# A decoder's quantised feed-forward on one Trainium2 core: int16 roundings, a stationary column of maxima, columns by token half, and constant products in TensorE's rests

## What is computed

```python
def _L0_ffn_ref(x, w_gate, w_up, w_down):        # x: 1024 tokens x 128
    def act_qdq(x):                              # one scale for the whole tensor
        qmax = 2.0 ** (ACT_BITS - 1) - 1.0       # 32767
        scale = jnp.maximum(jnp.max(jnp.abs(x)) / qmax, 1e-12)
        return jnp.clip(jnp.round(x / scale), -qmax - 1.0, qmax) * scale
    def fixed_qdq_u16(x):
        scale = 1.0 / 65536.0
        return jnp.clip(jnp.round(x / scale), 0.0, 65535.0) * scale
    x = act_qdq(x)
    up = act_qdq(x @ lpbq_dequant(w_up).T)       # 384 x 1024 results
    gate = act_qdq(x @ lpbq_dequant(w_gate).T)
    sig = fixed_qdq_u16(jax.nn.sigmoid(gate))
    gate = act_qdq(gate * sig)
    o = act_qdq(gate * up)
    return o @ lpbq_dequant(w_down).T
```

## Time and profile before

| | |
|---|---|
| median of 3 runs | 481.63 us (478.5 to 483.13) |
| the profiled execution's own time | 481.88 us |
| its span (first to last instruction) | 480.1 us |
| VectorE busy | 335.9 us, 70% |
| TensorE busy | 320.3 us, 67% |
| ScalarE busy | 194.4 us, 40% |
| mean granted TensorE clock | 0.83 |

### The profile page before, as it was taken

One profiled execution on the slowest core, in us unless ns is written; L12 is line 12 of the kernel. 1 busy time (PEld: TensorE's weight loads), 2 busy tenths in 40 slices (PEclk: granted clock), 3 DMA queues, 4 the chain that ended last, 5 costly groups with the idle time before them and its releaser, 6 DMA issues.

```text
span 480.1 us, 8901 instructions
## 1 busy us (share of the span) xinstructions
PE 320.3 (67%) x3651; PEld 197.5 (41%) x3651; DVE 335.9 (70%) x479; ACT 194.4 (40%) x310; POOL 90.0 (19%) x86
## 2 busy tenths in 40 slices
PE   2605779767666575799999973920095998789821
PEld 0201233222222334477777761400033777467710
DVE  0796899999999955666666644488833674666574
ACT  1519968546445330122222252475113442434420
POOL 0070033444343403400000000000003341112000
PEclk9856799888899597699999996765576798989965
DMA  8600000000005768100000000000000000000001
GB/s 236 255 0 16 1 1 22 23 22 22 1 21 101 132 117 286 73 3 1 3 1 3 3 1 0 0 0 1 0 0 0 3 4 3 1 2 5 3 0 44
DMA packets 22500, 16.91 MB, mean 35 GB/s; under 512 B 17216, under 2 KB 20416, under 8 KB 22336
## 3 DMA queue, kind: packets, MB, share of 16 engines
q1 hardware_dynamic: 22464, 16.39, 12.5%
HBM read 11.67 MB, written 4.72 MB: 34 GB/s over the span
## 4 chain that ended last, share of the span: by engine, by line
PE 36%; DVE 19%; SPq 6%; issue 5%; ACT 3%; DMA 1%; POOL 0%; DVEq 0%; ACTq 0%; POOLq 0%
PE psum L441 29%; SPq L423 6%; PE psum L699 3%; DVE small L1455 2%; DVE arena_a L1397 2%; PE psum L581 2%; PE psum L548 2%; DVE small L1539 1%; DVE arena_a L1417 1%; ACT arena_b L1050 1%; DMA g_scratch<-arena_a 1%; DVE arena_b L1510 1%; DVE arena_b L1516 1%; DVE arena_b L1543 1%; DVE xc L1220 1%
## 5 line engine op out<-in xcount | busy, mean ns | idle before, releaser
L441 PE MATMUL psum<-arena_b 64*64 64x9 f32 (+2 forms) x1348 | 75.3, 278 | 43.8 <-DVE arena_b L1364 30.6
L441 PEld LDWEIGHTS psum<-arena_b 64*64 64x64 f32 (+2 forms) x1348 | 34.9, 141 | 73.6 <-issue 38.8
L441 PE MATMUL psum<-arena_a 64*64 64x64 f32 (+2 forms) x1056 | 34.8, 235 | 9.0 <-ACT arena_a L904 5.4
L1539 DVE TENSOR_REDUCE small<-psum 128x16 f32<-128x1024 f32 x16 | 19.6, 1225 | 20.2 <-PE psum L441 20.2
L441 PEld LDWEIGHTS psum<-arena_a 64*64 64x64 f32 (+1 forms) x1056 | 21.9, 139 | 28.5 <-issue 15.8
L1148 POOL TENSOR_TENSOR arena_b<-arena_b 128x512 f32<-128x512 f32 x16 | 24.8, 1551 | 43.3 <-DVE arena_b L1334 43.3
L441 PE MATMUL psum<-arena_a,xw 128*128 128x128 f32 x256 | 31.1, 279 | 2.4 <-ACT arena_a L969 2.2
L441 PEld LDWEIGHTS psum<-arena_a,xw 128*128 128x128 f32 x256 | 30.1, 195 | 4.0 <-ACT arena_a L969 2.7
L441 PE MATMUL psum<-arena_b,const 32*128 32x128 f32 (+1 forms) x138 | 9.1, 346 | 32.3 <-DVE arena_b L1462 32.0
L1172 POOL MEMSET arena_b<- 128x16 f32 x4 | 0.3, 128 | 160.1 <-DVE x L1529 160.1
L1145 POOL TENSOR_TENSOR arena_b<-arena_b 128x512 f32<-128x512 f32 x16 | 21.9, 1369 | 44.0 <-DVE arena_b L1351 44.0
(11 more groups left out here) (218 smaller groups left out, 731.1 us busy)
## 6 DMA issues: line engine op xcount, KB each, us to landing
g_scratch<-arena_a SPq DMA_DIRECT2D x16, 256.0 KB, 6.6
logg<-g_scratch SPq DMA_DIRECT2D x1, 3584.0 KB, 13.2
xw<-in_xw SPq DMA_DIRECT2D x1, 2048.0 KB, 9.1
arena_b<-in_rkvo SPq DMA_DIRECT2D x8, 192.0 KB, 2.3
ffn_w<-in_ffn SPq DMA_DIRECT2D x1, 576.0 KB, 10.8
x<-in_xT SPq DMA_DIRECT2D x2, 256.0 KB, 3.0
arena_a<-in_boxes SPq DMA_DIRECT2D x8, 64.0 KB, 4.0
arena_b<-in_rkvo SPq DMA_DIRECT2D x8, 64.0 KB, 1.9
```

Source lines behind the costliest of these rows:

```text
L441: return nc.tensor.matmul(o, l, r, start=start, stop=stop, **kw)
L1539: v_.tensor_reduce(mx.rearrange("p (r h) -> p r h", r=4), s4, axis=AX.X, op=ALU.max).then_inc(s.a_max, 1)
```

## The change

Five edits, all in the feed-forward.

1. The roundings of gate, up and gate times sigmoid are single passes that write int16; the scaled sigmoid is written as uint16. The multiplies read these integers and write float32. Four integer tensors lie in an area of SBUF that the cross attention has left.
2. The broadcast uses the column of maxima itself, repeated 128 times, as stationary operand and the identity as moving operand. `f_diag` and its pass are gone. In `scale_of` a one-column operation before the broadcast (`per`) takes the factor in; all rounds then have the same three operations behind the reduce.
3. Columns are ordered by token half first: piece h * 3 + j. The first three gate products need only half 0 of x, whose subtraction VectorE makes; ScalarE makes half 1's.
4. VectorE reduces the gate's products from PSUM, and ScalarE copies a bank after VectorE is done with it. Up is reduced in one pass over 3072 columns. The down products start chunk by chunk, half 1's roundings are all ScalarE's, and the last scale is applied in the residual add.
5. `keep_running(n)` issues n products of constants (mean matrix by 512 columns of `xw`) into `pD`'s first bank, which nothing reads then: 3 before round 0's broadcast, 2 behind it, 4 before round 2's, 2 before rounds 3 and 4, 1 behind round 4's.

```diff
@@ tensor @@
             def spread_max(n):
                 pe.wait_ge(s.f_amax, n + 1)
-                mm(pD[:, 512:640], mean_w, f_diag).then_inc(s.f_bc, 1)
+                mm(pD[:, 512:640], small[:, 0:1].to_broadcast([P, P]), ident).then_inc(s.f_bc, 1)
+
+            def keep_running(n):
+                for _ in range(n):
+                    mm(half(pD, 0), mean_w, xw[:, 0:512])
+
+            keep_running(3)
             spread_max(0)
-            pe.wait_ge(s.f_q3, 1)
+            keep_running(2)
...
-                    mm(banks[j], ffn_wT[:, (k * HID + j // 2) * P:(k * HID + j // 2 + 1) * P],
-                       half(fx, j % 2)).then_inc(s.h_psum, 1)
+                    elif j == 0:
+                        pe.wait_ge(s.fx_done, 1)
+                    elif j == HID:
+                        pe.wait_ge(s.fx1_done, 1)
+                    w = k * HID + j % HID
+                    mm(banks[j], ffn_wT[:, w * P:(w + 1) * P], half(fx, j // HID)).then_inc(s.h_psum, 1)
...
-            for n in range(2, 5):
-                spread_max(n)
-            for h in range(2):
-                pe.wait_ge(s.h_o, h + 1)
+            keep_running(4)
+            spread_max(2)
+            pe.wait_ge(s.f_mid, 1)
+            keep_running(2)
+            spread_max(3)
+            pe.wait_ge(s.f_mid, 3)
+            keep_running(2)
+            spread_max(4)
+            keep_running(1)
+            for h in range(2):
                 for j in range(HID):
...
+                    pe.wait_ge(s.h_o1 if h else s.h_o, j + 1)
@@ scalar @@
+            act.wait_ge(s.fx_big, 2)
+            nc.scalar.activation(half(fx, 1), half(fx, 1), ACT.Identity, bias=der[:, 30:31]).then_inc(s.fx1_done, 1)
...
-                act.wait_ge(s.f_q3, 2 + i)
-                nc.scalar.activation(sig[:, columns], gate[:, columns], ACT.Sigmoid, scale=small[:, 10:11])\
+                act.wait_ge(s.gate_q, 1 + i)
+                nc.scalar.activation(piece(sig, i), piece(gate_q, i), ACT.Sigmoid, scale=small[:, 21:22])\
                     .then_inc(s.h_sig, 1)
                 act.wait_ge(s.h_sig, 1 + i)
-                nc.scalar.activation(sig[:, columns], sig[:, columns], ACT.Identity, scale=65536.0, bias=der[:, 29:30])\
-                    .then_inc(s.sig_up, 1)
+                nc.scalar.activation(piece(sig_q, i), piece(sig, i), ACT.Copy, scale=65536.0).then_inc(s.sig_q, 1)
...
@@ vector, scale_of @@
-                v_.tensor_scalar(f_diag, ident, small[:, 0:1], None, ALU.mult).then_inc(s.f_amax, 1)
+                v_.tensor_scalar(per, factor, 1.0 / QMAX16, None, ALU.mult).then_inc(s.f_amax, 1)
...
                 link(v_.tensor_reduce(inv, pD[:, 512:640], axis=AX.X, op=ALU.max))
...
+                link(v_.tensor_scalar(sc, inv, per, 1e-12, ALU.mult, ALU.max))
+                link(v_.reciprocal(rec, sc))
+                v_.tensor_scalar(use, rec, factor, None, ALU.mult).then_inc(s.f_rec, 1)
@@ vector, the stage @@
...
+            for i in range(2):
+                v_.tensor_scalar(piece(gate_q, i), piece(gate, i), use, None, ALU.mult).then_inc(s.gate_q, 1)
+            dve.wait_ge(s.h_done, 4 * HID)
+            link(amax(up))
+            s_up, use = scale_of(2, 1, s_x16)
             for i in range(2):
...
+                dve.wait_ge(s.sig_q, i + 1)
+                dve.wait_ge(s.gate_q, 2)
+                link(v_.scalar_tensor_tensor(piece(gate, i), piece(sig_q, i), 1.0 / 65536.0, piece(gate_q, i),
+                                             ALU.mult, ALU.mult))
+                amax(piece(gate, i), 1 + i).then_inc(s.f_mid, 1)
...
+            v_.tensor_scalar(piece(gate2_q, 0), piece(gate, 0), use, None, ALU.mult)
...
+            v_.tensor_tensor(piece(sig, 0), piece(gate2_q, 0), piece(up_q, 0), ALU.mult)
+            dve.wait_ge(s.gate2_q, 1)
+            v_.tensor_tensor(piece(sig, 1), piece(gate2_q, 1), piece(up_q, 1), ALU.mult).then_inc(s.f_mid, 1)
...
+            for j in range(HID):
+                v_.tensor_scalar(half(gate, j), half(sig, j), use, MAGIC, ALU.mult, ALU.add).then_inc(s.o_big, 1)
+                dve.wait_ge(s.o_big, j + 1)
+                v_.tensor_scalar(half(gate, j), half(gate, j), MAGIC, None, ALU.subtract).then_inc(s.h_o, 1)
             for h in range(2):
                 dve.wait_ge(s.h_psum, 4 * HID + h + 1)
-                v_.tensor_tensor(half(x, h), half(x, h), half(pA, h), ALU.add).then_inc(s.x3_done, 1)
+                v_.scalar_tensor_tensor(half(x, h), half(pA, h), s_o, half(x, h), ALU.mult, ALU.add).then_inc(s.x3_done, 1)
```

## The result

| | before | changed |
|---|---|---|
| median of the first comparison, 4 runs each | 480.4 us (478.5 to 483.13) | 463.34 us (461.67 to 466.81) |
| ratio | | 0.9649, 95% interval 0.9585 to 0.9713 |
| profiled execution, its span | 481.88, 480.1 us | 461.67, 459.9 us |
| VectorE / TensorE / ScalarE busy | 335.9 / 320.3 / 194.4 us | 328.2 / 329.5 / 195.4 us |
| mean granted TensorE clock | 0.83 | 0.87 |

The change made the kernel 3.5% faster. All twelve runs of the changed kernel that this study has lie between 461.67 and 467.67, with a median of 464.5.

The account below looks back on a forecast made before the run. VectorE's linked chain of passes was taken as the bound, with TensorE starting both product groups at 1.2 GHz. 481.88 less 2.85 (part 1) and 10.7 (parts 2 to 5) gave 468.3 us; forecast 465.5 to 471, range 464.5 to 473.

Parts of the forecast that it names:

- Part 1: Feed-forward up to the end of the sixth gate product: gain 2.85 us from six products at the higher TensorE level.
- Part 2: From the gate products to the up scale: fewer rounding passes and a single reduce of up, gain 2.95 us.
- g: The end of the sixth gate product, 308.92 us in the kernel before; later times are counted from it.
- Part 3: Gate times sigmoid: gain 2.05 us more, ScalarE's sigmoid in time, VectorE going on at g + 20.55 after round 3.
- Part 4: Products of the roundings, shared by VectorE and ScalarE: VectorE goes on at g + 30.7, before g + 37.14.
- Part 5: Down products, started by chunks at the higher level: last residual add ends at g + 37.8, 4.3 us gained here.
- Layer norm and attention "move with it one to one": Behind the last residual add: layer norm and attention wait for it and shift by the same amount.
- A: Rival at gate and down products: constants do not raise TensorE's level, total 475.3 us; 6 in 100.
- B: Rival at the rounding passes: 16-bit writes go at the rate of two-source passes, 470.3 us; 8 in 100.
- C: Rival at the multiplies: 16-bit ones go in pairs, 466.7 us, or 465 with rounds 3 and 4 high; 10 in 100.
- D: Rival: every pass touching int16 takes twice a two-source pass, 13.6 us more, 481.9, no change; 4 in 100.
- E: Rival: TensorE's level stays at 1.2 GHz from 292 to 357 us, constants in the way, 488.9 us; 2 in 100.

Follow-up runs that it names:

- the third profile: The changed kernel profiled again with nothing changed; broadcasts of rounds 3 and 4 ran at 1.2 GHz; stage 48.06 us, 122.84 us behind it.
- the maxima from SBUF: The changed kernel with gate's maxima again taken from ScalarE's copies in SBUF: 465.48 us, stage 48.06.

## Why the forecast was right in the stage and wrong in sum

- **Part 1, up to g.** Forecast 2.85, between 2.0 and 3.4. From the first maximum to the end of the sixth gate product it is 13.20 before (295.72 to 308.92) and 10.08 after (292.76 to 302.88 less 0.04): 3.1. The sum is right, two of its terms are not, and they offset each other in part. The constants never held the broadcast up: it starts 1.70 after the first maximum, not 2.3, and the first gate product comes 0.5 sooner than before, where I had said at the same time. And the six gate products take 5.4 from the first's start, not 5.15. The level was even up before the constants in this profile (1.12 for the squares' product, for 1.64). In the third profile they began at 1.2 GHz; the level rose 4.0 us after the squares' product began, not 5.1, and the first gate product came no later.
- **Part 2.** Forecast g + 11.2 for the multiply by the sigmoid, measured 314.09 - 302.84 = g + 11.25. The last up copy decides, by 0.16. Right, and so is that round 1 gains nothing from the earlier maximum, as the maxima from SBUF show.
- **Part 3.** Forecast g + 20.55 behind round 3; measured 323.15 = g + 20.3, at the high level, and 0.3 later in the third profile. Nothing waits for ScalarE's sigmoid. Right in its times. That VectorE needs no clamp rests on the uint16 write holding the scaled sigmoid at 65535, which no run shows; what the runs show is that each clamp costs 0.96 where it stands.
- **Part 4.** Forecast g + 30.7; 333.00 = g + 30.2. The 0.5 is the level in rounds 3 and 4, which I had put in the range; the third profile, with both at the lower level, has g + 30.8. 16-bit passes cost what I took from the bfloat16 row. Right.
- **Part 5.** Forecast g + 37.8; measured 340.21 = g + 37.4. The residual add with the scale takes 0.75, not 0.69, which is 0.06 on the path. Right.
- **Layer norm and attention "move with it one to one".** This is the step that failed. Behind the stage the changed kernel has 119.7 to 122.8, mean 120.8, before 122.6: 1.8 us less on average, 3.0 in the first profile, for a term that the forecast had at nothing. I had taken TensorE's level for something that the stage gains from inside and had not asked in what position it hands the level on. The low stretches behind the stage, 20.5 us, could be seen in the trace of before; what they cost shows only beside the other profiles, 3 us for 10 us.
- **The range.** It took the spread of three runs around a centre of 468.3. The measured 463.34 is 5.0 below it. The failed step accounts for 1.8 and the stage for 0.45. Two more are chance: I counted from an execution of 481.88, and the median of before beside the changed kernel is 480.4, 1.5 lower; and unchanged code in front of the stage was 1.1 shorter on average. The four runs were lucky too: the median of all twelve is 464.5. Without the failed step the four runs would lie inside the range, near 465.1. The twelve runs lie at its edge with it: the range was too narrow on the fast side, for a kernel whose unchanged first 295 us vary by 6.5 us.
- **Rivals.** A: the constants do raise the level. B, C and D: passes to int16 take 1.02 and multiplies 1.76; none of them came. On C the Trainium skill (VectorE: DVE Perf Modes, What auto-detection actually checks) says that a two-source operation gets the double rate only if every tensor is 16 bit. The trace agrees: two int16 sources with a float32 result take 1.76 for 1536 columns, the time of float32. E: the level rose.
- For PSUM sources the Trainium skill (VectorE: DVE Perf Modes, The TRN2 errata) gives a fixed term 62 cycles larger than for SBUF. The trace does not agree: a reduce of 512 columns took 0.69 from PSUM (302.88) and 0.69 from SBUF in the kernel before (six of them, 303.64 to 309.59).

## What to carry to other kernels

Constant products in TensorE's rests pay when they have raised the level and it holds until the real products are done: three of them were worth 2.9 us here. A rest of 2.2 us between them and the down products lost most of the gain in one profile (7.11 for 5.42) and none in another (5.42), so read the granted clock on both sides of the rest instead of trusting its length. When an edit changes TensorE's level at the end of a stage, count the stages behind it as touched too, and look in the trace for their low stretches. Here, rounding by writing an integer type saved whole passes and cost nothing in the passes that read it. And before moving a maximum earlier, look whether its broadcast stands behind other products in TensorE's queue.

## What the runs showed of the hardware that I had not expected

- Unchanged code took between 291.45 and 297.98 us to the first maximum, in seventeen profiles.
- The stretch behind the stage, with the same instructions and VectorE busy for 73.3 us, took 119.7 to 122.8 us in one and the same kernel, going with 10.2 to 20.5 us of TensorE at 1.2 GHz.
- After a rise at 345.0 and a rest of 2.2 us, TensorE's level fell in the kernel before with all constants (7.11 for six down products) and held in the one with constants around round 4 only (5.42).
- A stationary operand that repeats one column 128 times costs TensorE what the diagonal form costs: the broadcast takes 0.49 alone and 0.38 in a stream with either.
- `tensor_scalar` from float32 to int16 takes 1.02 for 1536 columns, a multiply of two int16 tensors into float32 1.76, the times of float32. ScalarE's pass over 3072 columns into int16 takes 2.84, where its two float32 passes took 2.95 and 2.86.
